# New instruction orders for one step on ScalarE, VectorE, GpSimd and SyncE in an adapter-then-linear kernel (32 samples, one core)

## What is computed

```python
w1 = W1[language_ids]; w2 = W2[language_ids]
h = relu(einsum('bsh,bha->bsa', x, w1) + b1[language_ids][:, None, :])      # 512 -> 128
adapted = einsum('bsa,bah->bsh', h, w2) + b2[language_ids][:, None, :]      # 128 -> 512
y = x + adapted
mean = mean(y); var = mean(square(y - mean))
normed = (y - mean) * rsqrt(var + 1e-05)
x1 = x + normed * gamma[language_ids][:, None, :] + beta[language_ids][:, None, :]
out = x1 + einsum('bti,bio->bto', x1, W[cat_ids]) + b[cat_ids][:, None, :]
```

## Time and profile before

| | us |
|---|---|
| median of 3 runs | 614.54 (614.09 to 615.64) |
| the profiled execution | 615.36 |
| its span, first to last instruction | 613.5 |
| matmul instructions busy | 605.9 (99% of the span) |
| weight loads busy | 490.3 (80%) |
| VectorE, ScalarE, GpSimd busy | 520.5, 514.2, 525.7 (85%, 84%, 86%) |
| granted TensorE clock | 1.000 |

### The profile page before, as it was taken

How to read it: one execution, slowest core, us unless ns; L and a number is a source line. 1 busy time by engine, 2 the same in 40 slices (tenths; PEclk the granted TensorE clock), 3 DMA queues, 4 the chain that set the end, 5 groups by cost and what they waited for, 6 DMA issues and landing times.

```text
span 613.5 us, 10721 instructions
## 1 busy us (share of the span) xinstructions
PE 605.9 (99%) x2866; PEld 490.3 (80%) x2866; DVE 520.5 (85%) x1151; ACT 514.2 (84%) x772; POOL 525.7 (86%) x265
## 2 busy tenths in 40 slices
PE   9998999999999999999999999999999999999998
PEld 7766888778888888888888888778888888888887
DVE  1889889789898888988989899898898888899673
ACT  4978888789888899888889889889888989889770
POOL 5789998799989999888998889899888998989830
PEclk9999999999999999999999999999999999999999
DMA  9987899878998888899898997989999898997422
GB/s 305 236 273 247 299 317 286 268 257 264 309 301 272 285 284 274 300 289 301 252 303 255 311 295 257 296 265 289 309 289 291 261 296 263 314 308 269 160 87 104
DMA packets 125939, 166.24 MB, mean 271 GB/s; under 512 B 11062, under 2 KB 72768, under 8 KB 121812
## 3 DMA queue, kind: packets, MB, share of 16 engines
q1 hardware_dynamic: 94900, 150.12, 75.0%
q10 hardware_dynamic: 30912, 15.73, 9.2%
q0 software_dynamic: 96, 0.05, 0.0%
HBM read 132.17 MB, written 33.55 MB: 270 GB/s over the span
## 4 chain that ended last, share of the span: by engine, by line
PE 86%; DMA 4%; SPq 3%; DVE 3%; ACT 2%; issue 2%; POOL 0%; ACTq 0%; DVEq 0%; POOLq 0%
PE o_bank L833 17%; PE o_bank L835 17%; PE o_bank L834 17%; PE n_bank L851 8%; PE d_bank L833 5%; PE d_bank L835 5%; PE d_bank L834 5%; PE d_bank L876 4%; DMA x_quad<-in_x 2%; PE y_bank L833 2%; PE y_bank L835 2%; PE y_bank L834 2%; DMA x_tok<-in_x 2%; SPq L243 1%; DVE xT L666 1%
## 5 line engine op out<-in xcount | busy, mean ns | idle before, releaser
L833 PE MATMUL o_bank<-w_hi,x1T_hi 128*128 128x512 f32 x512 | 205.4, 401 | 1.8 <-DVE x1T_lo L731 1.8
L835 PE MATMUL o_bank<-w_hi,x1T_lo 128*128 128x512 f32 x512 | 200.0, 391 | 0.0
L834 PE MATMUL o_bank<-w_lo,x1T_hi 128*128 128x512 f32 x512 | 199.1, 389 | 0.0
L666 DVE STREAM_TRANSPOSE xT<-x_quad 128x512 f32<-128x512 f32 x120 | 127.2, 1102 | 38.7 <-DMA x_quad<-in_x 38.7
L428 POOL TENSOR_TENSOR w_lo<-w_raw,w_hi 128x1024 fp32r<-128x1024 f32 x62 | 149.3, 2408 | 10.5 <-ACT w_hi L511 10.4
L501 ACT ACTIVATE norm<-y,neg_mean_rstd,rstd 128x512 f32<-128x512 f32 x128 | 151.8, 1262 | 1.1 <-DVE neg_mean_rstd L716 1.1
L423 POOL TENSOR_TENSOR x_tok<-x_tok,b_bc 128x1024 f32<-128x1024 f32 x60 | 145.0, 2417 | 4.5 <-issue 2.6
L518 ACT ACTIVATE x1T_hi<-n_bank,params 128x512 fp32r<-128x512 f32 x126 | 85.2, 690 | 35.3 <-DVE n_bank L725 26.9
L833 PEld LDWEIGHTS o_bank<-w_hi,x1T_hi 128*128 128x128 f32 x512 | 96.3, 188 | 21.7 <-issue 3.8
L835 PEld LDWEIGHTS o_bank<-w_hi,x1T_lo 128*128 128x128 f32 x512 | 96.1, 188 | 21.0
L834 PEld LDWEIGHTS o_bank<-w_lo,x1T_hi 128*128 128x128 f32 x512 | 96.4, 188 | 17.8
(11 more groups left out here) (95 smaller groups left out, 818.0 us busy)
## 6 DMA issues: line engine op xcount, KB each, us to landing
w_raw<-in_L_cond_W SPq DMA_DIRECT2D x32, 1024.0 KB, 6.5
out<-out_half SPq DMA_DIRECT2D x63, 512.0 KB, 4.6
x_tok<-in_x SPq DMA_DIRECT2D x31, 1024.0 KB, 11.5
w_raw<-in_L_cond_W SPq DMA_DIRECT2D x64, 256.0 KB, 4.3
b_bc<-in_L_cond_b SPq DMA_DIRECT2D x64, 256.0 KB, 8.6
x_quad<-in_x SPq DMA_DIRECT2D x62, 256.0 KB, 3.7
x_quad<-in_x ACTq DMA_DIRECT2D x58, 256.0 KB, 10.7
x_tok<-in_x ACTq DMA_DIRECT2D x2, 256.0 KB, 3.3
```

The source lines that it names most:

```text
L666: dve.transpose(xT[(k.x + 1) % 3][:, c, :].rearrange("p (b j) -> p b j", j=SQ), x_quad[1 - k.b][:, :, c::NC]).then_inc(xT_done, 1)
L833: pe.matmul(acc, lhs_hi, rhs_hi, start=first, stop=False)
L834: pe.matmul(acc, lhs_hi, rhs_lo, start=False, stop=False)
L835: return pe.matmul(acc, lhs_lo, rhs_hi, start=False, stop=last)
```

## The change

Nothing is computed differently. What moves:

- ScalarE: `normalise` of three tiles stands ahead of the first half of `w_hi`, the fourth between the halves. `w2_hi` stands ahead of `relu`, and `xs_hi` and `w1_hi` behind it, ahead of x1's chunks 0 and 1 (in step 2 behind them). All four squares and the root stand ahead of x1's chunks 2 and 3. Its two quarter loads are gone.
- VectorE: the statistics stand ahead of `low_x1` of chunks 2 and 3.
- GpSimd: the first b2 pair stands ahead of `plus_identity`, both halves of `w_lo` behind the second pair, `xs_lo` ahead of `w1_lo`.
- SyncE: all four quarter loads are issued at its step's start; the second half's store moves into the next step, and the parameter row stands ahead of the first half's store. Three parameter rows in place of two (`params[k.x]`), so the row's load waits for a sample earlier.

```diff
 # SyncE
-            def load_x_quads(s, p, quads=(0, 1)):
-                for n in quads:
+            def load_x_quads(s, p):
+                for n in range(NQ):
...
                     load_x(k.sample(-1), q)
+                if linear and k.since(3):
+                    store(k, 3, 1)
                 if turn:
...
                     load_b(cat_b, q)
+                if loads:
+                    if k.since(2):
+                        sp.wait_ge(x1_lo_done, k.count(NC, 1, 0))
+                    load_params(lang, (k.x + 1) % 3)
                 if linear:
                     store(k, 2, 0)
-                if loads:
-                    sp.wait_ge(x1_lo_done, k.count(NC, 0, 0))
-                    load_params(lang, q)
-                if linear:
-                    store(k, 2, 1)
 # GpSimd
+                    if adapter and not k.last(2):
+                        plus_b2_pair(0)
                     if turn:
                         plus_identity()
-                    if adapter:
+                    if adapter and k.last(2):
                         plus_b2_pair(0)
-                    if turn:
-                        low_w_pair(0)
                     if adapter:
                         plus_b2_pair(2)
                     if turn:
+                        low_w_pair(0)
                         low_w_pair(2)
                 if follow:
                     low_w2(q, k.count(1, -1, 1))
                     if k.since(2):
+                        low_xs(k)
                         low_w1(k)
-                        low_xs(k)
 # ScalarE
                 k = Step(h, p)
-                if k.last(2):
-                    for t in range(NT):
-                        normalise(k, t)
-                    high_w(k, 0)
-                else:
-                    high_w(k, 0)
-                    for t in range(NT):
-                        normalise(k, t)
+                for t in range(NT - 1):
+                    normalise(k, t)
+                high_w(k, 0)
+                normalise(k, NT - 1)
                 high_w(k, 2)
+                if follow:
+                    high_w2_of_next(k)
                 if adapter:
                     relu(k)
-                if follow and not k.last(S - 2):
-                    load_next_x_quads(k)
+                if follow and not k.last(2):
+                    high_xs_of_next(k)
+                    high_w1_of_next(k)
                 high_x1(k, 0)
                 high_x1(k, 1)
-                if follow:
-                    high_w2_of_next(k)
+                if k.last(2):
+                    high_xs_of_next(k)
                     high_w1_of_next(k)
-                    high_xs_of_next(k)
                 if adapter:
-                    square(k, 0)
-                    square(k, 1)
-                    square(k, 2)
+                    for t in range(NT):
+                        square(k, t)
+                    deviation(k)
                 high_x1(k, 2)
                 high_x1(k, 3)
-                if adapter:
-                    square(k, 3)
-                    deviation(k)
 # VectorE
                 x1(k, 2)
                 x1(k, 3)
+                if adapter:
+                    variance(k)
+                    inverse_deviation(k)
                 low_x1(k, 2)
                 low_x1(k, 3)
                 output(k, 3)
-                if adapter:
-                    variance(k)
-                    inverse_deviation(k)
```

More of the change, by code:

```diff
@@ L22, in pairs, with thirds @@
         return ROUND // 2 * self.h + (self.p - back) // 2
+    def thirds(self, back):
+        return ROUND // 3 * self.h + (self.p - back) // 3
     def count(self, per, back, more):
@@ L99, in adapter_then_conditional_linear @@
         b_bc = [sb(f"b_bc{i}", [P, H]) for i in range(2)]
-        params = [sb(f"params{i}", [P, NP]) for i in range(2)]
+        params = [sb(f"params{i}", [P, NP]) for i in range(3)]
         x_quad = [sb(f"x_quad{i}", [P, NB, NC * SQ]) for i in range(2)]
@@ L184, in adapter_then_conditional_linear @@
         b2_in = [sem(f"b2_in{i}") for i in range(2)]
-        params_in = [sem(f"params_in{i}") for i in range(2)]
+        params_in = [sem(f"params_in{i}") for i in range(3)]
         w_in = [sem(f"w_in{i}") for i in range(2)]
@@ L338, in _ @@
                          ).then_inc(first_b1_in[1], 16)
-            load_x_quads(2, 0, range(NQ))
+            load_x_quads(2, 0)
             sp.wait_ge(table_done, 1)
@@ L357, in _ @@
             last = Step(S // ROUND, 3)
+            store(last, 3, 1)
             store(last, 2, 0)
@@ L557, in step @@
                 k = Step(h, p)
-                if k.last(2):
-                    for t in range(NT):
-                        normalise(k, t)
-                    high_w(k, 0)
-                else:
-                    high_w(k, 0)
-                    for t in range(NT):
-                        normalise(k, t)
+                for t in range(NT - 1):
+                    normalise(k, t)
+                high_w(k, 0)
+                normalise(k, NT - 1)
                 high_w(k, 2)
+                if follow:
+                    high_w2_of_next(k)
                 if adapter:
                     relu(k)
-                if follow and not k.last(S - 2):
-                    load_next_x_quads(k)
+                if follow and not k.last(2):
+                    high_xs_of_next(k)
+                    high_w1_of_next(k)
                 high_x1(k, 0)
                 high_x1(k, 1)
-                if follow:
-                    high_w2_of_next(k)
+                if k.last(2):
+                    high_xs_of_next(k)
                     high_w1_of_next(k)
-                    high_xs_of_next(k)
                 if adapter:
-                    square(k, 0)
-                    square(k, 1)
-                    square(k, 2)
+                    for t in range(NT):
+                        square(k, t)
+                    deviation(k)
                 high_x1(k, 2)
                 high_x1(k, 3)
-                if adapter:
-                    square(k, 3)
-                    deviation(k)
-            def load_x_quads(s, p):
-                for n in (2, 3):
-                    act.dma_start(x_quad[p][quad(n), :, :],
-                                  x_quads[bass.ds(s, 1), n].rearrange("o j b f -> j (o b) f")
-                                  ).then_inc(xq_in[p], 16)
-            def load_next_x_quads(k):
-                act.wait_ge(xT_done, k.count(NC, 0, NC))
-                load_x_quads(k.sample(-2), k.b)
             act.dma_start(x_tok[0][:, 1, :], x_rows[0, :, 1, :]).then_inc(first_x_in[1], 16)
@@ L731, in low_x1 @@
                 dve.scalar_tensor_tensor(x1T_lo[q][:, c, :], norm_bank(k, c)[:, :],
-                                         params[q][:, NC + c:NC + c + 1], x1T_hi[q][:, c, :].bitcast(F32),
+                                         params[(k.x + 2) % 3][:, NC + c:NC + c + 1], x1T_hi[q][:, c, :].bitcast(F32),
                                          ALU.add, ALU.subtract).then_inc(x1_lo_done, 1)
```

13 lines of the change are left out of this document (6 added, 7 removed).

## The result

| | before | after |
|---|---|---|
| median, us | 614.56 (614.09 to 615.64) | 658.21 (657.07 to 658.95) |
| ratio | 1 | 1.0703, 95% interval 1.0676 to 1.0729 |
| span of the profiled execution | 613.5 | 655.4 |
| granted TensorE clock | 1.000 | 0.997 |

The change makes the kernel 7% slower. I forecast 652.5 us, 6.2% slower, with a range of 637 to 662.

What follows compares the result with a forecast made beforehand. TensorE's own matmuls, 18.40 us a step, were taken to bound the kernel. Steps 34.7, step 32 0.3, old waits -1.9 and step 2 4.9 add 38.0 us to 615.36, making 653.4; median 652.5, range 637 to 662.

Steps and rivals of the forecast that it cites:

- The loop that decides: Round through TensorE, ScalarE and VectorE: grows from 17.80 to 19.64 us, so TensorE waits 1.24 us in every step.
- c2: TensorE's third chunk of linear_tile(k, 0), which waits for the low part of x1's chunk 2 from the step before.
- The sum: Whole kernel: 34.7 + 0.3 - 1.9 + 4.9 = 38.0 us slower.
- the wait per step: TensorE's wait in steps 4 to 31: 28 x 1.24 = 34.7 us more.
- the mark: The start of up on TensorE, once a step; predicted to come every 19.6 us instead of 18.40.
- Step 2: W2's copy ahead of relu waits there for its just-issued load, taken to land in 4.3 us: 4.9 us more.
- How much slack there was: Old loop of 17.80 us against TensorE's step of 18.40: 0.60 us of slack.
- item 1: From relu, through hT_hi, xs_hi, W1's part and x1T_hi, to chunk 0's low part: R+3.71 against R+3.20.
- statistics alone: Rival, chance 0.13: copies ahead of x1's first parts cost nothing; loop 19.13, wait 0.73 a step, 638 us.
- At nothing: Terms costed at zero: normalise ahead of W's parts, GpSimd's order, SyncE's stores and parameter rows.
- The cover that I named for the norms: On ScalarE before the next relu: 0.5 us, beyond which each delay costs one for one.
- The rule of the Trainium skill: Rival, chance 0.01: weight loads' share of 80% leaves TensorE a fifth open; better orders save 72 us, about 542.

Runs made afterwards that it cites:

- e14_parts_store_first: Kernel after, with xs_hi and W1's part behind x1's first pair and the previous step's second-half store right behind W1 and W2: 629.25 us, ratio 1.0236.
- e3_w2_step2: Kernel after, with W2's copy put behind relu in step 2 alone: 656.19 us, ratio 1.0653.
- e7_norm_back: Kernel after, with the norms put back behind W's first half: 687.88 us, ratio 1.1182.
- e12_sync_alone: Kernel before, with the change's whole SyncE part (quarters, stores, parameter rows) and the old orders on the other engines: 677.08 us, ratio 1.0986.
- e11_stores: Kernel after, with the second half's store back at the end of its own step: 826.03 us, ratio 1.3421.
- e6_before_spquads: Kernel before, with ScalarE's two quarter loads moved to SyncE at its step's start with the other two: 623.69 us, ratio 1.0141.
- e13_before_quads_late: Kernel before, with all four quarter loads on SyncE behind the other loads and the first store: 639.55 us, ratio 1.0359.
- e10_parts_stores: Kernel after, with xs_hi and W1's part behind x1's first pair and the second half's store in its own step: 809.61 us, ratio 1.3143.

## Why the prediction was right, and where its working was not

**The loop that decides: right.** The step is bound by `c2`, `relu`, x1's first pair, y, the squares, the root, the statistics, x1's low part of chunk 2, and `c2`. Working and measurement, from the start of `relu`:

| | predicted | after |
|---|---|---|
| low part of chunk 0 | 3.71 | 3.70 |
| root | 10.17 | 10.06 |
| reciprocal | 10.50 | 10.39 |
| low part of chunk 2 | 11.39 | 11.28 |
| TensorE | 12.29 | 12.17 |
| with TensorE's part of the loop | 19.64 | 19.47 |

The 0.11 lies between y and the root: the four squares start 0.71 apart, and I took 2.24 for three intervals plus 0.83 for the root, where it is 2.98. The rest are hundredths in TensorE's part, 7.30 for 7.35.

**The sum: near, partly by luck.** The span grew by 41.9 us where I had 38.0. Three pieces were off: the wait per step, 4.8 us too much; an excess over it that I did not have, 6.05; and step 2, 2.7 too little. The first nearly cancels the second.

**28 steps: 34.06 us, against 34.7 - 1.9 = 32.8.** The floor of 1.07 a step gives 30.0, less the 1.94 of old waits 28.0, and 6.05 us come on top, in steps of 19.5 to 20.7. I had the floor 0.17 too high, which is the 4.8 us, and this excess at nothing. VectorE waited 2.4 us in all for stores, in five steps, and these are the five longest (20.71, where it waited 1.16, and 19.91 to 20.16). Most of the remaining 3.6 us is not the store: e14_parts_store_first has no such wait and still takes 3.3 us over its floor. In both kernels two small delays make it up, `relu` 3.20 behind the mark in place of 3.11 in 9 steps, and x1's low part of chunk 2 later by 0.09 in the steps of the middle. What causes these stays open.

**Step 2: mis-sized, 7.6 for 4.9,** and outside the 0 to 6 that I had given it. W2's load was issued 1.1 us later than I had it, since the prologue was already 0.9 later, and it landed after 6.15 us, not 4.3: ScalarE goes on at 46.34, and the chain of waits has the load from 40.17 for 6.15. The 4.3 was the middle of 64 loads, W1's and W2's, over the whole kernel; here 1 MB of x went out just ahead. e3_w2_step2 adds that taking W2's copy out of the way in step 2 wins nothing that lasts.

**How much slack there was: wrong, and not seen in the sum.** I read the old loop in the step at 168.54, where the low part of chunk 0 starts at 3.20 behind `relu`. VectorE had waited 1.82 us for the quarters of x in that step. In the 28 steps this start lies anywhere from 2.55 to 4.72. In a quiet step, with the quarters of x nearly in time, it starts at 2.57, and chunk 2's at 9.02. ScalarE and VectorE of the kernel before, in the step whose `up` begins at 555.44:

```profile
558.67 0.64 ACT L528 ACTIVATE d_bank<-d_bank,params 128x512 f32<-128x512 f32 x1
```

```profile
561.24 1.60 DVE L731 SCALAR_TENSOR_TENSOR x1T_lo<-n_bank,params,x1T_hi 128x512 fp32r<-128x512 f32 x2
...
567.69 1.42 DVE L731 SCALAR_TENSOR_TENSOR x1T_lo<-n_bank,params,x1T_hi 128x512 fp32r<-128x512 f32 x2
```

With 0.89 to TensorE and 7.30 behind, the old loop is 17.21 there, so its slack was 1.19 and not 0.60. The steps of the change, from quiet steps of three kernels:

| | low part of chunk 2 behind `relu` | loop |
|---|---|---|
| before | 9.02 | 17.21 |
| e14_parts_store_first: statistics first | 10.37 | 18.56 (steps from 18.55) |
| after: `xs_hi` and W1's part ahead too | 11.28 | 19.47 |

The statistics add 1.35, where I had 1.33. The copies ahead of x1's first pair add 0.91 where I had 0.51. The sum came out right because item 1 was built forwards from `relu` and did not use the old start; only the slack and the split were taken from a disturbed step. So the rival "statistics alone" was priced wrongly as well: its own loop is 18.55, a wait of 0.15 a step and not 0.73. With the slack of 1.19 the statistics alone cost this loop 0.15 a step; the two copies make it 1.07. I had it the other way round, most of it from the statistics.

**"At nothing": true, of the three terms tried, of GpSimd's order only.** The norms' place is worth 29.7 us (e7_norm_back). SyncE's part costs 62.7 us alone (e12_sync_alone), and in the change its store's move is needed, because without it W2 would be late (e11_stores). The cover that I named for the norms, 0.5 us, was near: ScalarE waits 0.70 for TensorE in front of `relu`. What I did not ask was what ScalarE's round takes with each part absent. I looked for one loop where there were two, within about a microsecond of each other. The sum was not hurt, because the cover was worked out for the new order; but the norms' move, counted at nothing, is what gives this cover.

**The rule of the Trainium skill.** I weighed the Trainium skill's page Perfetto Trace Analysis (Identifying the Most-Contended Engine), by which the weight loads' share tells how much TensorE has open; it names MFU (the share of the peak rate of arithmetic) beside it, which I did not work out. The share is 80% before, but 28 steps differ from 28 x 18.40 us by 1.94 in all, and in none of the runs was a steady step clearly below 18.40 us. By this case's runs 80% was already full for these orders, and the distance between marks was the view to trust.

## What to carry to other kernels

Follow every loop that is near the bound, not only the one that the change lengthens: each in-order engine's own round through its program is one, and a move that is free in one loop may be what keeps another short. Take the durations of a loop from a quiet step, and compare two steps before you call a difference slack. When a store or load moves on a queue, ask what large transfers now stand ahead of it and which buffer waits for it; parts of a change that looked independent here were harmless only together.

## What the runs showed that I had not expected

- A store of 512 KB landed in 3.2 to 3.5 us when issued ahead of the loads of W and x (e14_parts_store_first), in 2.8 to 4.1 when issued some 12 us behind them (the second half's, before), and in 9.2 to 13.2 when issued right behind them (before, after, e12_sync_alone), all read between 280 and 420 us of the traces. The place in SyncE's order moved its landing by far more than the loop's slack.
- Moving two issues from ScalarE to SyncE was not neutral. The page DMA: Bandwidth & Descriptors of the Trainium skill (Issuing engines are not separate DMA queues) says that issuing from several engines only saves the issuing time. e6_before_spquads and e13_before_quads_late, slower by 1.4% and 3.6%, show that when a load goes out and what it stands behind matter too: W1 and W2 landed in 5.2 us in the first, against 4.3 before.
- VectorE's 38.7 us of waits for x, the largest wait of before that looked like a loss, cost the 28 steps 1.94 us at most. Half of that is one step of 19.42 (from 112.00): VectorE waited 3.44 us for the quarters ahead of it, and TensorE then for the low part of h. Taking the waits away by moving the loads, e6_before_spquads, made the kernel slower.
- In e10_parts_stores and e11_stores, with TensorE waiting some 5 us in every step, the mean granted clock of the traced run was 0.914 and 0.907 of full speed. In the traced runs of all other kernels it was 0.982 or more, and 0.977 in one run more of e12_sync_alone. So a part of the loss of these two kernels may be slower matmuls; it was not taken apart.
